# Attention on eight images: row maxima from the rounded parts of q and k alone, two half-array products side by side every second step

## The reference

```
q = Wq xf + bq          (64 x 1024)
k = Wk xf + bk          (64 x 1024)
v = Wv xf + bv          (128 x 1024)
attn = softmax(q^T k)   (1024 x 1024, rows are queries)
out = v attn^T          (128 x 1024)
result = gamma * out + x
```

## Time and profile before

| | |
|---|---|
| runs | 248.56 us median of 3 (247.63 to 250.33) |
| profiled execution | 247.75 us, of which the span from the first to the last instruction is 246.0 us |
| granted TensorE clock | 0.997 of full speed (the level of 2.4 GHz) |
| PE busy | 233.6 us, 95% of the span |
| ACT busy | 189.0 us, 77% |
| POOL busy | 176.5 us, 72% |
| DVE busy | 170.7 us, 69% |
| max matmuls L468 on `work` | 120 |

### The profile page before, as it was taken

One profiled execution on the slowest core, in us unless ns is written; L12 is line 12 of the kernel. 1 busy time (PEld: TensorE's weight loads), 2 busy tenths in 40 slices (PEclk: granted clock), 3 DMA queues, 4 the chain that ended last, 5 costly groups with the idle time before them and its releaser, 6 DMA issues.

```text
span 246.0 us, 4933 instructions
## 1 busy us (share of the span) xinstructions
PE 233.6 (95%) x1738; PEld 200.3 (81%) x1738; DVE 170.7 (69%) x287; ACT 189.0 (77%) x359; POOL 176.5 (72%) x158
## 2 busy tenths in 40 slices
PE   7998988999999999999999999999999999999992
PEld 7365867888879898898879888898888889898891
DVE  1667295876888767776878767877768767784354
ACT  2868956788787888779877887788877878879841
POOL 8578986299963897469962898558982877668760
PEclk9999999999999999999999999999999999999998
DMA  4706400570409312390407504191105601010102
GB/s 97 237 29 145 113 0 4 128 173 3 128 0 223 79 45 87 85 217 0 131 0 174 129 0 129 34 229 40 45 0 124 177 3 45 0 45 0 44 15 73
DMA packets 8040, 19.85 MB, mean 81 GB/s; under 512 B 1744, under 2 KB 2256, under 8 KB 8016
## 3 DMA queue, kind: packets, MB, share of 16 engines
q1 hardware_dynamic: 7776, 19.50, 30.3%
q10 hardware_dynamic: 240, 0.03, 0.1%
HBM read 4.33 MB, written 4.19 MB: 35 GB/s over the span
## 4 chain that ended last, share of the span: by engine, by line
PE 88%; ACT 5%; DVE 5%; issue 1%; POOL 0%; POOLq 0%; DVEq 0%; ACTq 0%
PE sums L529 24%; PE sums L545 12%; PE scores L510 12%; PE work L468 11%; PE scores L511 11%; PE work L462 5%; PE work L478 3%; DVE qk_lo L731 2%; ACT qk_hi L643 2%; PE work L473 2%; PE sums L559 2%; PE work L457 1%; PE work L456 1%; PE work L455 1%; DVE neg_max L740 1%
## 5 line engine op out<-in xcount | busy, mean ns | idle before, releaser
L392 POOL TENSOR_TENSOR weight_lo<-weight,weight_hi 128x512 bf16<-128x512 f32 x90 | 124.5, 1402 | 48.6 <-ACT weight_hi L679 48.2
L740 DVE TENSOR_REDUCE neg_max<-work 128x1 f32<-128x512 f32 x120 | 81.7, 686 | 25.5 <-PE work L468 25.3
L676 ACT ACTIVATE weight<-scores 128x512 f32<-128x512 f32 x128 | 76.6, 599 | 22.6 <-PE scores L511 18.9
L529 PEld LDWEIGHTS sums<-values,weight_hi 128*128 128x128 f32 x512 | 78.1, 188 | 9.9 <-issue 0.5
L529 PE MATMUL sums<-values,weight_hi 128*128 128x258 f32 x512 | 81.7, 282 | 0.1
L679 ACT ACTIVATE weight_hi<-scores 128x512 fp32r<-128x512 f32 x128 | 76.5, 597 | 0.0
L510 PE MATMUL scores<-q_hihi,k_hilo 128*128 128x512 f32 x128 | 55.1, 430 | 1.2 <-ACT weight_hi L679 1.1
L511 PE MATMUL scores<-q_lomax,k_hione 128*128 128x512 f32 x128 | 50.4, 394 | 0.0
L468 PE MATMUL work<-k_hilo,q_hihi 128*128 128x512 f32 x120 | 48.6, 411 | 1.7 <-DVE qk_lo L731 0.9
L779 DVE TENSOR_TENSOR weight_lo<-weight,weight_hi 128x512 bf16<-128x512 f32 x38 | 35.7, 940 | 2.4 <-ACT weight_hi L679 2.4
L545 PE MATMUL sums<-values_b,weight_lo 128*128 128x130 bf16 x512 | 35.5, 221 | 0.0
(11 more groups left out here) (78 smaller groups left out, 186.4 us busy)
## 6 DMA issues: line engine op xcount, KB each, us to landing
out<-y_sb SPq DMA_DIRECT2D x15, 256.0 KB, 2.5
x_sb<-in_x SPq DMA_DIRECT2D x7, 512.0 KB, 4.4
q_hihi<-qk_hi SPq DMA_DIRECT2D x14, 256.0 KB, 4.4
k_hilo<-qk_hi SPq DMA_DIRECT2D x7, 256.0 KB, 3.1
k_hilo<-qk_lo SPq DMA_DIRECT2D x7, 256.0 KB, 5.1
q_lomax<-qk_lo SPq DMA_DIRECT2D x7, 256.0 KB, 5.2
k_hione<-qk_hi SPq DMA_DIRECT2D x7, 256.0 KB, 5.1
x_sb<-in_x SPq DMA_DIRECT2D x2, 256.0 KB, 3.5
```

Of the source, the lines that this page charges most:

```text
L392: pool.tensor_tensor(weight_lo[:, r], weight[:, r], weight_hi[:, r], ALU.subtract).then_inc(weight_lo_pool_done, 1)
L529: last = pe.matmul(sums[:, it, 0:VCOLS], weight_hi[:, r, tile(it)], values[p][:, j], start=(j == 0), stop=False)
L676: act.activation(weight[:, r], scores[:, s % 2], ACT.Exp)
L740: dve.reduce_max(neg_max[:, h, t:t + 1], place, AX.X, negate=True).then_inc(neg_max_done, 1)
```

## The change

From batch 1 on (image n > 0), a max product takes q_hi and k_hi alone, over 64 partitions. The keys of the first half stay where they are, in partitions 0 to 63 of `k_hilo`, and those of the second half are copied to partitions 64 to 127 of a new tensor `k_up`; with the two copies of q_hi in `q_hihi`, the products for the two key halves use the upper and lower 64 rows of the array. The two jobs of one query tile are issued in a pair, in every even step; odd steps have none. The job `out` of each chunk moves one step earlier. `spread` gets one DMA more (128 KB); the DMA of k_lo is counted in `spread_rest`, which becomes three. Steps 0 to 10 of batch 0 keep their order.

```
-SPREAD_MX, SPREAD_REST = 4, 2
+SPREAD_MX, SPREAD_REST = 4, 3
...
-    chunk = (s + 12) // TILES
-    return [(chunk, (s + 12) % TILES)] if chunk < CHUNKS else []
+    chunk, i = divmod(s + 12, TILES)
+    return [(chunk, i), (chunk, i + 1)] if chunk < CHUNKS and i % 2 == 0 else []
...
-    if k == 6 and b > 0:
+    if k == 5 and b > 0:
         jobs.append(("out", 2 * b - 1, 0))
...
-    if k == 14:
+    if k == 13:
         jobs.append(("out", 2 * b, 0))
...
+        k_up = [sbuf(f"k_up{p}", [128, CHUNK], fp32r) for p in range(2)]
...
                 sp.dma_start(q_hihi[p][HEAD:2 * HEAD, :].bitcast(fp32), qk_hi[0:HEAD, :].bitcast(fp32)).then_inc(spread_mx[p], 16)
+                sp.dma_start(k_up[p][HEAD:2 * HEAD, :].bitcast(fp32),
+                             qk_hi[HEAD:2 * HEAD, chunk(1)].bitcast(fp32)).then_inc(spread_mx[p], 16)
                 sp.wait_ge(qk_lo_done, half_count(n, HALVES - 1))
-                sp.dma_start(k_hilo[p][HEAD:2 * HEAD, :].bitcast(fp32), qk_lo[HEAD:2 * HEAD, :].bitcast(fp32)).then_inc(spread_mx[p], 16)
+                sp.dma_start(k_hilo[p][HEAD:2 * HEAD, :].bitcast(fp32), qk_lo[HEAD:2 * HEAD, :].bitcast(fp32)).then_inc(spread_rest[p], 16)
...
             def max_scores(n, t, h, place):
                 p = n % 2
-                pe.matmul(place, q_hihi[p][:, tile(t)], k_hilo[p][:, chunk(h)], start=True, stop=True).then_inc(mx_done, 1)
+                if n == 0:
+                    pe.matmul(place, q_hihi[p][:, tile(t)], k_hilo[p][:, chunk(h)], start=True, stop=True).then_inc(mx_done, 1)
+                else:
+
+                    rows = slice(h * HEAD, (h + 1) * HEAD)
+                    keys = k_hilo[p][0:HEAD, chunk(0)] if h == 0 else k_up[p][HEAD:2 * HEAD, :]
+                    pe.matmul(place, q_hihi[p][rows, tile(t)], keys, start=True, stop=True).then_inc(mx_done, 1)
```

## The result

The changed kernel takes 285.61 us in the median of 4 runs (284.85 to 286.23), the kernel before 248.09 us beside it (247.48 to 250.33). The ratio is 1.149, 95% interval 1.141 to 1.157. The profiled execution took 285.27 us with a span of 283.4 us; the granted clock is 0.999 of full speed, so the clock has no part in it. The forecast was 276 us.

What follows compares the result with a forecast made beforehand. The prediction took TensorE's own instruction sequence as the bound. 247.75 us (profiled kernel before) + 25.4 for the waits + 3.3 for changes of shape = 276.4, forecast as 276 us, range 266 to 286.

Steps and rivals of the forecast that it cites:

- ten free pairs: Pairs not waiting for a side job, seven in step 0, two in batch 0, one in batch 6; each gains 0.24 us.
- the waits: Pairs' second halves and `mt` wait for bank readers on TensorE: +4.28 us a steady batch, +25.4 us net of overlap gains.
- the relays: Time from a `qk`, `v` or `out` job's matmul, through its readers, to the waiting second half of a pair.
- the array's change of shape: Switches between whole-array and half-array matmuls on TensorE's path: 66 at 0.05 us, +3.3 us; at 0.16, +10.6 us.
- the array emptied at each change: Rival: waits as forecast, but each shape switch drains the array, 284 us; chance 0.27, shared with `ACT` being late.
- relief: Restart of 0.34 us behind the 39 waiting pairs might already hold 0.11 of each switch: 4 us less, 280 us.
- the likeliest case: Forecast proper: the waits as worked out, and 0 to 0.08 us per shape switch; chance 0.62.
- The halves aren't side by side: Rival: a pair's two half-array matmuls run serially, so ten free pairs lose 0.24 us each: 279 us, inside the forecast.
- the free pair of step 0: Pair in a batch's step 0 that waits for no side job: 0.24 us gained by overlap, before two switches at 0.05.
- ACT late: Rival: ACT reads each `qk` and `v` job 0.3 us late, +7 us, 284 us; chance 0.27, shared with array emptying.
- TensorE passing the waiting half: Rival: TensorE goes on with `sums_hi` while a bank is read, keeping the 13 us overlap gain: 231 us; chance 0.04.
- At nothing: Items put at no cost: the DMA to `k_up`, `out` a step earlier, DVE's reductions, ACT and POOL.

Runs made afterwards that it cites:

- e1: New job order alone (pairs in even steps, `out` one step earlier), whole-array products, on the kernel before: 275.44 us against 248.19, ratio 1.108.
- e3: Changed kernel with every half-array pair computed twice into the same two banks once both are free: 303.39 us, ratio 1.223 to the kernel before.
- e2: Changed kernel with the job order of before, half-array products issued one in a step: 287.37 us against 248.19 for the kernel before, ratio 1.158.
- e4: Kernel before with whole-array max pairs in odd steps, ahead of the same step's side job, `out` in steps 5 and 13: 263.33 us, ratio 1.060.
- e8: Kernel before with odd chunks' max jobs later: none in steps 12 and 13, two in step 14; `out` of step 14 moved to 15: 256.17 us, ratio 1.032.
- e6: Changed kernel's order with every pair computed twice, but as whole-array products: 314.52 us against 248.06 for the kernel before, ratio 1.267.

## Why the prediction was right, and where it was short

**The bound and the mechanism** were right: TensorE's own sequence sets the time, six of eight pairs wait for the side job of the step before, and nothing behind passes them. e1 gives it alone: 27.3 us measured, 27.8 by the prediction's numbers (25.4, and 2.4 for the ten free pairs, whose products don't overlap there). By its steady batches the waits were put about 1.5 us too high, partly because max jobs of before had waits of 0.04 us that the prediction left out.

**The waits, one by one**: 1.96, 2.52 and 1.45 us for the relays against 1.96, 2.52 and 1.44; in number 12, 14 and 13 in the list of waits against 13, 13 and 13. The relay of `mt` on its own pair took 129.37 - 128.09 = 1.28 against 1.17; the half before it lasts 0.50, not 0.39. The prediction's 13 waits on qk_lo and 13 on the values were a slip against its own list of pairs, which has 12 and 14.

**The term that was mis-sized is the array's change of shape.** The prediction took 0.05 us for each of 66 changes and 0.16 as the upper bound; it is 0.20, above that bound. The bound had the later start only; the weight load that is no longer ahead of its matmul was not in it. And the row it leaned on (from a 128*1 product to a whole one, 0.05) was not a like case. With the measured sizes: 39 waited pairs x (0.42 + 0.58 - 0.34 - 0.475) = 7.2; ten free ones x 0.385 = 3.9; seven steps with `mt` x (0.09 + 0.11) = 1.4; 12.5 instead of 3.3, or 0.19 for each of the 66. The sum becomes 247.75 + 25.4 + 12.5 = 285.7, and 285.27 was measured. So the time is that of the rival "the array emptied at each change" without its relief (284 us), and the likeliest case, given 0.62, was not what happened. The relief (280 us, if the restart already holds 0.11 of each leaving change) did not come: a waited pair pays 0.19 more than a waited whole one, the whole price of leaving. Only the entering change hides in the wait and the restart, as the prediction had counted.

That 285.61 us lies inside the range of 266 to 286 is luck in part. It is 0.4 us from the upper end, and the waits put 1.5 us too high made up for some of the 9 us that the change of shape was put too low.

The Trainium skill's rule (TensorEngine Tiling, Key Properties), that changing the tiling mode drains the TensorE, agrees with e3 in that the cost comes at the two changes, with one pair between them or two; that the array is emptied, no run shows.

**The halves aren't side by side**: refuted by the free pairs, 0.00 us apart, and by e2, where a single half takes as long as a pair. The gain of 0.24 is real, and each of those pairs pays 0.39 for it. That is also a step the prediction had with the wrong sign: the free pair of step 0 was to gain 0.24 less 0.10, and it loses 0.15.

**ACT late, and TensorE passing the waiting half**: neither was seen. The relays are as long as in batch 0 of before, and L538 starts behind the waiting half in every pair.

**At nothing**: the DMA to `k_up` cost nothing that shows. In the waits list of the changed kernel no matmul waits for it.

What stays open: why a weight load at a change of shape starts only with its own matmul, about 1 us of e2, and why DVE's `weight_lo` took 2.57 us once in e1 and in e4.

## What to carry to other kernels

Where engines share a few banks in turn, write out the list of jobs and ask of each how many steps lie between the job that fills a bank and the one that takes it next; a relay through two engines took 2 to 2.5 us here, and a reordering that shortens that distance costs more than the matmul it saves. If the kernel has one stretch with the new order already (here batch 0), its rows give the price. Half-array pairs pay only if several stand between two changes of shape: here the estimate is 1.7 pairs, and with two banks there is one.

## What the runs showed of the hardware

- A change between whole-array and half-array matmuls cost TensorE 0.20 us at a granted clock of 0.99 to 1.0 (the 2.4 GHz level): about 0.09 ahead of it and 0.11 behind; the weight load of the new shape started with its own matmul instead of 0.23 us ahead of it. A half-array matmul of 512 columns in between ran at the speed of a whole one (0.39 us; 128.01 to 128.34 in e3 is 0.23 and the 0.10 of the seam), and two on different row halves started within 0.04 us of each other.
- DVE's operation on four columns, L747, takes 0.16 us at its shortest in the kernel before and took 0.97 while POOL ran a subtraction on SBUF (e4), ending with it; DVE's `weight_lo` takes 0.68 at its shortest and took 1.76 in e8. The Trainium skill (SBUF — State Buffer, SBUF: two separate sides) has a port pair that a DVE operation with two SBUF inputs and a POOL operation that reads SBUF lock against each other for a whole instruction; the ends in e4 agree (151.23 and 151.20), but no run here took POOL's operation away.
- In two runs the granted clock fell behind a wait: in e1 TensorE stood still from 32.67 to 34.76, and from 36 to 38 us the clock was 0.50 (1.2 GHz), from 39 on 1.00 again. In e4 a wait of 2.10 us in the same place had the same behind it, in e6 one of 2.00 us had not (1.00 throughout).
